# A decoder layer on one core: where the gate's statistics are formed, and the gated mixing batch by batch

## The reference

```python
q, k, v = (silu(dwconv_causal(x @ w.T, conv)) for each)   # 4 taps; 4 heads of 64
beta = sigmoid(x @ b_w.T)
delta = delta_rule(l2norm(q), l2norm(k), v, beta)          # chunks of 32 tokens, state 64 x 64 per head
short, long_, wide = fir(v, fir_s), fir(v, fir_l), fir(v, fir_wd)   # 3, 31 and 64 taps per channel
# _stats(t): per token and head the mean, the root mean square and the largest magnitude of 64 channels
gate_in = concat([x, _stats(short), _stats(long_), _stats(wide), _stats(delta), _stats(v)])
logits = gelu(gate_in @ g1_w.T + g1_b) @ g2_w.T + g2_b     # 512 hidden; 5 logits per head
p = softmax(logits)                                         # with a temperature; floor f
o = (f + s*p0) * short + (f + s*p1) * long_ + (f + s*p2) * wide + (f + s*p3) * delta + s*p4 * v
o = o * rsqrt(mean(o * o) + 1e-5) * onorm_w                # over the 64 channels of a head
x1 = layernorm(x + o @ o_w.T)
```

## Time and profile before

| | us |
|---|---|
| runs of the kernel before: median of 3 | 763.48 |
| lowest, highest | 762.04, 767.56 |
| profiled execution, its own time | 764.04 |
| profiled execution, span of the core | 762.3 |
| mean granted clock of TensorE | 0.93 of full |
| stage one | 0 to 56.8 |
| stage two | 56.8 to 338.9 |
| stage three | 338.9 to 501.0 |
| stage four (cross attention), five (feed-forward) | 501.0 to 640.0, to 762.3 |

### The profile page before, as it was taken

One profiled execution on the slowest core, in us unless ns is written; L12 is line 12 of the kernel. 1 busy time (PEld: TensorE's weight loads), 2 busy tenths in 40 slices (PEclk: granted clock), 3 DMA queues, 4 the chain that ended last, 5 costly groups with the idle time before them and its releaser, 6 DMA issues. The chain is left out here.

```text
span 762.3 us, 17132 instructions
## 1 busy us (share of the span) xinstructions
PE 624.7 (82%) x7348; PEld 446.4 (59%) x7348; DVE 448.7 (59%) x878; ACT 302.3 (40%) x739; POOL 131.3 (17%) x96
## 2 busy tenths in 40 slices
PE   5746799999989988866867894859999974999884
PEld 2532577777677777652346443748778763555543
DVE  2674567377567555349984445443346684566765
ACT  2664345445445444255511340112232424444441
POOL 0001700600520240100224134252200011000000
PEclk9787989999999999996988997979999986999998
DMA  5104401500410320212000204230000000000001
GB/s 172 41 0 144 135 3 54 161 14 10 161 58 3 103 96 4 85 45 94 28 1 0 83 1 167 72 111 1 0 1 1 0 1 0 1 1 29 28 1 56
DMA packets 26536, 37.48 MB, mean 49 GB/s; under 512 B 4641, under 2 KB 13602, under 8 KB 26463
## 3 DMA queue, kind: packets, MB, share of 16 engines
q1 hardware_dynamic: 26463, 36.41, 14.7%
HBM read 34.30 MB, written 2.10 MB: 48 GB/s over the span
## 5 line engine op out<-in xcount | busy, mean ns | idle before, releaser
L258 DVE SCALAR_TENSOR_TENSOR arena<-bank,conv_w,arena 128x511 f32<-128x511 f32 (+2 forms) x72 | 53.1, 746 | 28.9 <-ACT arena L364 17.7
L1237 POOL COPY arena<-v_win 128x256 f32<-128x256 f32 x32 | 21.7, 702 | 207.0 <-PE bank L600 206.9
L1884 ACT COPY arena<-bank 128x512 f32<-128x512 f32 x40 | 23.5, 586 | 73.3 <-PE bank L1769 38.5
L1769 PE MATMUL bank<-v_win,arena 128*128 128x256 f32 x192 | 45.7, 386 | 0.0
L600 PE MATMUL bank<-arena 128*32 128x128 f32 x512 | 35.6, 408 | 9.4 <-ACT arena L932 8.9
L2233 PE MATMUL bank<-v_win,arena 128*128 128x256 bf16 x288 | 36.5, 279 | 7.9 <-DVE arena L2320 6.9
L1769 PEld LDWEIGHTS bank<-v_win,arena 128*128 128x128 f32 x192 | 35.3, 190 | 8.6 <-issue 4.4
L937 ACT COPY arena<-bank 128x256 f32<-128x256 f32 x32 | 19.3, 604 | 52.7 <-PE bank L613 52.7
L573 PE MATMUL bank<-arena,qkv_w 128*128 128x512 f32 x64 | 32.3, 632 | 8.8 <-DMA arena<-in_xT 7.4
L2223 PE MATMUL bank<-arena,v_win 128*128 128x512 bf16 x144 | 36.3, 390 | 2.8 <-DVE arena L2291 2.8
L2233 PEld LDWEIGHTS bank<-v_win,arena 128*128 128x128 bf16 x288 | 28.4, 100 | 16.7 <-DVE arena L2320 7.9
(11 more groups left out here) (265 smaller groups left out, 1476.4 us busy)
## 6 DMA issues: line engine op xcount, KB each, us to landing
arena<-in_toep_w SPq DMA_DIRECT2D x32, 256.0 KB, 3.0
arena<-in_toep_l SPq DMA_DIRECT2D x32, 256.0 KB, 3.7
arena<-in_xT SPq DMA_DIRECT2D x12, 512.0 KB, 4.2
arena<-in_x SPq DMA_DIRECT2D x4, 512.0 KB, 5.4
arena<-in_ctx SPq DMA_DIRECT2D x4, 512.0 KB, 4.0
out<-arena SPq DMA_DIRECT2D x4, 512.0 KB, 2.9
qkv_w<-in_qkv_wT SPq DMA_DIRECT2D x1, 768.0 KB, 5.6
v_win<-in_w_gateT SPq DMA_DIRECT2D x1, 768.0 KB, 6.6
```

The costliest lines, as they stand in the source:

```text
L258: return nc.vector.scalar_tensor_tensor(out=acc[:, j:L], in0=src[:, 0:L - j], scalar=conv_w[:, m, CONV_K - 1 - j:CONV_K - j], in1=acc[:, j:L],
L1237: g.tensor_copy(A2["v_piece"][:, n % 2, :, :].rearrange("p c j -> p j c"), v_win[:, :, n * PIECE:(n + 1) * PIECE]).then_inc(s2["v_copied"] ...
L1769: i = mm(oo, src[:, k, f * P:(f + 1) * P], w[:, k, :], start=(k == 0), stop=(k == KT - 1 and f > 0))
L1884: nc.scalar.copy(dst(i), bank[n % RING].rearrange("p (t c) -> p t c", c=dst(i).shape[-1]))\
```

## The change

In stage one the loop over pairs is written out. The buffers of the stage move behind those of the filter matrices, so that xT of batch 0 for stage two and the first four filter matrices can be read at the end of stage one. The projections of batches 2 and 3 and ScalarE's first tap stand behind the turning of v of batches 0 and 1. ScalarE squares v and short; TensorE sums 64 channels of a head in products with the constant `heads`, and turns the sums to tokens, which ScalarE copies into `stats`:

```diff
+                def head_sums(b):
+                    pe.wait_ge(s1["v_squared"].sem, s1["v_squared"].at(b, 2))
+                    pe.wait_ge(s1["sh_squared"].sem, s1["sh_squared"].at(b, 2))
...
+                    rows = (a1["sh"], a1["sh_sq"], a1["vT"][:, :, DK:], a1["v_sq"])
+                    for j in range(4):
+                        for m in range(KT):
+                            for t in range(TT):
+                                i = nc.tensor.matmul(sums_bank(b)[COLS * t:COLS * (t + 1), 0:P], heads[:, m, 12 - 4 * j:12 - 4 * j + COLS],
...
                 def silus(b):
+                    if b >= 2:
+                        act.wait_ge(s1["sums"].sem, s1["sums"].at(b - 2, 1))
...
+                load_keys_xT(sp, 0)
+                for n in range(TOEP_BUFS):
+                    load_toep(sp, n)
...
+                for b0, b1 in pairs:
+                    turn_v(b0)
+                    turn_v(b1)
+                    if b1 + 2 < B:
+                        project(b0 + 2)
+                        project(b1 + 2)
+                    turn_short(b0)
+                    head_sums(b0)
+                    turn_short(b1)
+                    head_sums(b1)
+                    turn_sums(b0)
+                    turn_sums(b1)
```

In stage two `head_squares` goes, and of `statistic` only the largest values stay, both at level 2 of the inverse. Eleven jobs form the statistics of the filters (by head, all batches, once its eight pieces are done) and of delta (by batch), each one square of 128 x 1024 on ScalarE and three reduces on VectorE (1253, 1256 and 1260 are their lines):

```diff
+        OPENING, PER_ROUND = 8, 7
+        pieces_of = lambda b: range(OPENING + b * PER_ROUND, min(OPENING + (b + 1) * PER_ROUND, NPIECE))
+        fir_bank = lambda n: bank[5 if n < OPENING else 3]
+        JOBS = [(WIDE, 0), (LONG, 0), (DELTA, 0), (WIDE, 1), (DELTA, 1), (LONG, 1),
+                (DELTA, 2), (WIDE, 2), (LONG, 2), (WIDE, 3), (LONG, 3)]
...
                         elif more:
                             conv(b + 1, k - 3)
+                        elif k == 3:
+                            job_sum(6)
+                            job_largest(6)
...
                     rest(b, 1)
+                    j = 2 * b if more else 8
+                    job_sum(j)
+                    job_largest(j)
+                    job_squares(j)
+                    if more:
+                        job_sum(j + 1)
                     state_out(b, 1)
...
                     k_root(0)
+                copy_piece(5)
                 q_roots(0)
+                copy_piece(6)
                 v_scale(0)
+                copy_piece(7)
```

In stage three the statistics are there but for delta of batch 3 (`last_delta`). The stage is a pipeline over single batches with banks of its own for each step:

```diff
+                for b in range(B):
+                    if b:
+                        turn_o(b - 1)
+                        project(b - 1)
+                    if b < B - 1:
+                        logits(b + 1)
+                    mix(b, 0)
+                    if b < B - 1:
+                        turn_logits(b + 1)
+                    mix(b, 1)
+                    if b < B - 2:
+                        statistics(b + 2)
+                    mix(b, 2)
+                    mix(b, 3)
+                    if b < B - 2:
+                        for m in range(GH // P):
+                            hidden(b + 2, m)
...
+                for b in range(B):
+                    if b:
+                        residual(b - 1)
+                    if b < B - 1:
+                        softmax_before(b + 1)
+                    if b:
+                        shift(b - 1)
+                    if b < B - 1:
+                        softmax_after(b + 1)
+                        weigh(b + 1)
+                    head_sums(b)
+                    head_norm(b)
```

More of the change, by code:

```diff
@@ L260, in tap_one @@
                                                   op0=ALU.mult, op1=ALU.add)
+        pairs = [(2 * p, 2 * p + 1) for p in range(B // 2)]
         with nc.Block() as block:
@@ L864, in recurrence @@
                     state_part(b, 2)
-                    filter_piece(piece[4])
+                    if more:
+                        filter_piece(piece[4])
                     updates(b, 2, more)
@@ L985, in inverse @@
                             silu(b + 1, k - 3)
-                        head_squares(b, 3 * (k - 1), 3)
+                        if not more and k in (2, 3):
+                            square(k + 4)
                     for th in range(2):
@@ new lines, in _ @@
+                roots()
+                statistics_out(0)
+                a(A3[0]["sq_b"].rearrange("p (t h c) -> p t h c", t=TT, h=H), branch(DELTA, B - 1), ACT.Square).then_inc(s3["last_sq"].sem, 1)
+                for m in range(GH // P):
+                    gelu(0, m)
+                statistics_out(1)
+                logits_out(0)
+                gelu(1, 0)
+                gelu(1, 1)
+                exp(0)
+                gelu(1, 2)
+                gelu(1, 3)
+                for b in range(B):
+                    if b:
+                        turned_out(b - 1)
+                    if b < B - 1:
+                        logits_out(b + 1)
+                        exp(b + 1)
+                    if b:
+                        norm_out(b - 1)
+                    if b < B - 2:
+                        statistics_out(b + 2)
+                    mix_squares(b)
+                    if b < B - 2:
+                        for m in range(GH // P):
+                            gelu(b + 2, m)
@@ L1653, in _, with shift @@
-                statistics(0, 0, first=True)
-                statistics(1, 1, first=True)
-                for pair in range(B // 2):
-                    round_(pair, pair == 0, pair < B // 2 - 1)
+                def shift(b):
+                    u = b % 2
+                    dve.wait_ge(s3["ln_rs"].sem, s3["ln_rs"].at(b, 1))
+                    v.scalar_tensor_tensor(out=A3[u]["nm"], in0=A3[u]["mv"][:, :, 0], scalar=-1.0, in1=A3[u]["rs"],
+                                           op0=ALU.mult, op1=ALU.mult).then_inc(s3["nm_out"].sem, 1)
@@ new lines, in _ @@
+                small()
+                last_delta()
+                softmax_before(0)
+                softmax_after(0)
+                weigh(0)
+                for b in range(B):
+                    if b:
+                        residual(b - 1)
+                    if b < B - 1:
+                        softmax_before(b + 1)
+                    if b:
+                        shift(b - 1)
+                    if b < B - 1:
+                        softmax_after(b + 1)
+                        weigh(b + 1)
+                    head_sums(b)
+                    head_norm(b)
@@ L1658, in _ @@
+                residual(B - 1)
+                shift(B - 1)
             @block.gpsimd
@@ L1684, in layer @@
+                pool.wait_ge(s3["last_red"].sem, 5)
+                g.tensor_tensor(late_of(1), late_of(1), half_up, ALU.pow).then_inc(s3["last_root"].sem, 1)
+                weigh(0)
+                for b in range(B):
+                    if b:
+                        norm_roots(b - 1)
+                    if b < B - 1:
+                        weigh(b + 1)
+                    head_roots(b)
+                norm_roots(B - 1)
         PAIRS, PW = B // 2, 2 * COLS
```

800 lines of the change are left out of this document (424 added, 376 removed).

## The result

The changed kernel takes 771.26 us (median of 20 runs, 766.71 to 779.18) against 763.61 (758.07 to 769.05) of the kernel before, run beside it: a ratio of 1.0082, 95% interval 1.0059 to 1.0105. That is 0.8% slower, within the 1% that the prediction called the same, though the interval reaches just past it. Its profiled execution has a span of 769.6 us, 7.3 longer than before.

The account below looks back on a forecast made before the run. Stage two was held close to TensorE's own work, stage three had 45.5 us of idle TensorE, stage one a ScalarE chain. From 764.0, +15.1 + 2.3 - 17 and +0.6 for opening bursts gave 765.0 us, range 750 to 780.

Parts of the forecast that it names:

- prediction's own sign: Says the prediction is wrong if stage one grows by under 7 us, or stage three is under 135 or over 152.
- Stage one, forecast +15.1: Added squares, head sums and handovers: +6.9 to batch 2's silu, +6.7 in the second pair, 1.5 for lower clock.
- nothing behind them to cover: Stage one, second pair: squares 4.6 and sums 2.5 at its end count in full, less 0.4 of waits: +6.7.
- added 1.5 for the lower clock: Stage one: 1.5 us for part of the second pair's TensorE work at the lower clock, bounds 0 to 8.4.
- Opening, forecast +5.8: Stage two's start: early xT load -4.1; four more filter pieces 11.4, less 5.4 covered, plus 3.9 stall for POOL's power.
- Last inverse, forecast +1.7: Stage two: levels 3 to 5 carry two VectorE reduces each, 0.58 us a level.
- Last recurrence, forecast -5.2: Stage two: four pieces fewer on TensorE, -7.2, partly filled by three reduces a step; bounds -7.2 and 0.
- The removed squares of ScalarE: Stage two: removing 128 single-head squares gains 0, since TensorE's idle there goes mostly to VectorE.
- Rival B: Relieved ScalarE saves 2 us a round in stage two, or stage three nears TensorE's work: -8 to -14, about 754; chance 0.26.
- Stage three, forecast -17: Walk by TensorE checkpoints: hidden(0) at 5.7, mix 8.6, turning and projecting 8.5, end at 145 against 162.1; bounds -10, -26.
- Rival A: TensorE stays at the lower clock through stage one, its products take double: +8.4, 773.0; chance 0.2.
- Rival C: Weighing on VectorE and POOL bounds stage three, so idle only moves: -10 instead of -17, 772; chance 0.1.

Follow-up runs that it names:

- experiment 8: Kernel before, unread TensorE products added in stage three: 1.0064 with one set where there is no wait, then 0.9926 (760.2 us) with both in its waits.
- Experiment 5: Changed kernel without stage one's statistics of v and short: left out entirely, 0.989 of kernel before; formed in stage two as before, 0.993 (759.19 us).
- experiment 4: Changed kernel with POOL's copies of v moved ahead of the power in stage two's opening: piece 6 alone 1.0081, pieces 6 and 7 1.0017 of kernel before.
- experiment 1: Changed kernel with unread products (3, 8, 5) in TensorE's three waits of stage three: 0.9999 of kernel before.
- Experiments 1, 3 and 8: Number 3: changed kernel with batch 3's weighing of v behind batch 2's head sums, and unread products (3, 6, 5) in stage three's waits: 0.9938 of kernel before.
- experiment 9: Changed kernel with v and short statistics in stage two, both POOL copies ahead of the power, split weighing and unread products: 0.9787 of kernel before, 749.26 us.
- experiment 2: Changed kernel with the weighing of v of batch 3 moved behind the head sums of batch 2 in stage three: 1.0027 of kernel before.

## Why the prediction was right and wrong

The forecast of 765.0 against 771.3 was right in kind (a difference within 1%) and 6 us low. That it came so near is partly luck, since errors of opposite sign cancel: stage one came out 5.0 us below its forecast, stage two 2.3 above, stage three 8.4 above, and stages four and five 0.6 above the nothing that they had. By the prediction's own sign it is wrong in one part: it named a stage three of over 152 us as that sign, and 154.4 was measured.

*Stage one, forecast +15.1, measured +10.1.* The walk of the first pair holds: the silu of batch 2 starts at 47.71, with the whole stage begun 0.95 earlier, against 48.65. That early start is no part of the change: in experiment 8's kernels, with stage one as before, the first turning began at 20.5 us, in the changed kernel at 20.60, in the profile of the kernel before at 21.55. The second pair was over-sized: forecast +6.7, measured 4.1 (47.71 to 64.41, against 12.6 before). Up to the last copy of short it is 1.6 longer, though the eight squares take 4.6, and 2.6 follow for sums and turnings. Its squares lay partly in waits of ScalarE for TensorE that the step "nothing behind them to cover" had counted as full. The added 1.5 for the lower clock was not needed against a kernel before that had the same slow turnings. Experiment 5 gives the gross price of the statistics as 13.7, so the rest of the change gave 3.6 back (2.2 in the forecast). One thing that was read wrongly there: the prediction has a table load ahead of the silu of batch 2, covered by a wait. The changed kernel has none there. Its stage one loads tables at 11.79, 18.10 and 64.43, where the kernel before had two more, at 33.54 and 40.47, each of 1.28 us. In both kernels the next instruction starts 1.29 to 1.31 us after a load's start.

*Opening, forecast +5.8, measured +6.2.* The stall for the power was 3.67, forecast 3.9. The reason given, piece 6 behind the power, was true for the row and not enough for a cure (experiment 4).

*Last inverse, forecast +1.7, measured +5.6.* The step that priced an added reduce by two rows at full clock was right for itself (2.3 to 2.8 with the gaps). It had no term for the clock, which was 0.86 in the stretch and 1.00 before. The forecast's +0.6 for bursts at the lower clock stood for the opening alone.

*Last recurrence, forecast -5.2, measured -4.6* (333.2 to 353.9 against 313.3 to 338.6). *Added reduces in the other rounds, forecast 0*: the second `state_out` of a recurrence comes 10.7 us after the first in both kernels, so their cover held. *The removed squares of ScalarE, forecast 0*: experiment 5 bears it out within 3 us, for 31 us of ScalarE and eight reduces. Rival B's first half falls with it.

*Stage three, forecast -17, measured -8.6.* Every checkpoint of waits and order was within 0.5 us until the first mix, and all three waits were right in place and size. Behind them the walk falls short each time: the turning of o(2) starts at 114.6 (walk 112.7), that of o(3) at 138.2 (133.2), the end is at 154.1 (145). The failed step is the rate: "a mix of one batch 8.6", "8.5 for the turning and projecting" were read from rows at full clock and used behind waits of 3 to 9 us. At the full rate the products behind the three waits would have taken 2.9, 3.5 and 3.6 us less (the same steps in experiment 1 for the first, in the kernel before for the others). That is 10.0 together, enough for the whole miss of 9. The row that said otherwise stood among those quoted: 472.22 took 1.22 us for two instructions behind a wait of 9.76. Experiments 1, 3 and 8 show it in both kernels. That the row stood there does not mean that the size could be read from it: the clock behind waits differs between executions of the same code (experiment 9).

Rival A named the right mechanism at the wrong place. Its sum is 771.9 and not 773.0 (765.0, less the 1.5 us of the lower clock that the forecast holds already, plus 8.4), and that 771.3 was measured is luck. It put the lower clock into stage one, where the second pair was at 1.00, and not where the prediction itself had drawn new waits of 9 and 6 us. The Trainium skill's TensorE: Matmul & The Clock Gate, section Part 1: The HAM clock gate, says activity releases the clock from a throttled default; the traces agree as far as the windows behind waits go (0.52, 0.56, 0.61, and 1.00 in the first with the wait filled). Rival C foresaw the time (772) by another cause: weighing does not bound stage three as a whole, for TensorE works without a wait of over 1 us from 392.5 to 459.8. It does lengthen the one wait of 9 us, by the 1.5 us of experiment 2.

## What to carry to other kernels

When a walk leaves an engine idle for several microseconds ahead of matrix products, price the wait twice: once for itself, and once for what stands behind it at the lower clock, by rows behind waits in the trace at hand. Give the second price a range that starts at nothing: behind waits of 2.1 and 2.0 us the clock was 0.63 and 1.00 in two kernels here. Before moving work to "the engine that is free", ask in which stage it is free: the statistics of v and short cost 13.7 us in stage one, and in stage two at most about 3. And a slow operation of GpSimd belongs behind every short one that others wait for: moving one of two past it only moves the wait.

## What was not expected of the hardware

Products that nobody reads, put into real waits, made two kernels faster: 6 us of 771 in the changed one, 5.8 of 766 in the one before; put where there was no wait they cost their own time. They don't always hold the clock: behind a wait of which 2.1 us were left it was 0.63, though behind 2.0 us left it was 1.00 in the kernel before with fill. And while TensorE worked without a break from 320.5 to 326.0 us of the changed kernel, it had 0.50.

The same code of stage one took 66.8 to 67.3 us in four profiled executions and 62.6 and 63.0 in two others. The two first turnings of v, at 3.68 or 1.97 us each, make 3.4 us of that. And gaps of issue that sum to 1.1 to 3.4 us appeared in one dense stretch of small products, where the kernel before had 0.28 us; they were seen in every kernel built on the change, and their cause is open.

GpSimd's power over 128x16 took 2.90 us in the changed kernel, and 3.81 when a product of VectorE was moved beside it (experiment 2). That product in turn took 2.95 us beside GpSimd's weighing and 1.21 beside the power.
